# Scores as steps: each score bank keeps the scores of two key tiles ago

## The reference

```python
xq = einsum('bsh,oh->bso', x, wq).reshape(bsz, 16, seqlen, 64)   # k, v likewise
scores = softmax(einsum('bhid,bhjd->bhij', xq, xk) * SCALE)
out = einsum('bhij,bhjd->bhid', scores, xv).reshape(bsz, seqlen, 1024)
return einsum('bso,ho->bsh', out, wo)
```

## Time and profile before

| | us |
|---|---|
| median of three runs | 1537.33 (1533.9 to 1538.94) |
| the profiled execution, its own time | 1539.9 |
| its span, first to last instruction | 1538.1 |
| mean granted TensorE clock | 0.977 of full |

### The profile page before, as it was taken

The page is one execution under the profiler, slowest core; times in us unless marked ns, Lnnn a source line. Parts: engine busy times, 40 slices in busy tenths (PEclk is TensorE's granted clock), DMA queues, the critical chain, the costliest instruction groups (busy, mean ns, idle before and its releaser), DMA issues.

```text
span 1538.1 us, 23944 instructions
## 1 busy us (share of the span) xinstructions
PE 1475.9 (96%) x8778; PEld 803.9 (52%) x8778; DVE 936.0 (61%) x1017; ACT 650.2 (42%) x785; POOL 1197.4 (78%) x534
## 2 busy tenths in 40 slices
PE   5899999999999999999999999999999999998898
PEld 4455545555555555554555555554555555544555
DVE  4556666666556656666666656665666666665544
ACT  4344344444344434434444434443444444443432
POOL 1198988888789878898788878987988888976232
PEclk8799999999999999999999999999999999998999
DMA  6010101010101001010101010000101010000000
GB/s 166 1 28 1 28 1 28 1 29 1 29 1 28 1 5 25 1 28 1 28 1 28 1 29 1 15 15 1 28 1 28 1 28 1 1 1 0 8 7 14
DMA packets 22161, 24.71 MB, mean 16 GB/s; under 512 B 2730, under 2 KB 13618, under 8 KB 22066
## 3 DMA queue, kind: packets, MB, share of 16 engines
q1 hardware_dynamic: 21922, 23.28, 6.3%
q10 hardware_dynamic: 144, 0.00, 0.0%
HBM read 5.31 MB, written 1.05 MB: 4 GB/s over the span
## 4 chain that ended last, share of the span: by engine, by line
PE 83%; DVE 9%; issue 4%; POOL 2%; ACT 1%; SPq 1%; DMA 1%; DVEq 0%; POOLq 0%; ACTq 0%
PE ps L1081 26%; PE ps L1006 11%; PE ps L1056 7%; PE ps L1064 7%; PE ps L1059 7%; PE ps L1069 7%; PE ps L985 5%; DVE peak_parts L825 3%; DVE inv_sum L845 3%; PE ps L988 2%; PE ps L432 2%; PE ps L1105 2%; PE ps L433 2%; PE ps L414 2%; PE ps L1094 2%
## 5 line engine op out<-in xcount | busy, mean ns | idle before, releaser
L759 POOL TENSOR_TENSOR acc<-acc,probs 128x1024 f32<-128x1024 f32 x448 | 1075.5, 2401 | 159.8 <-ACT probs L712 129.7
L825 DVE TENSOR_REDUCE peak_parts<-ps 128x2 f32<-128x1024 f32 x512 | 624.4, 1221 | 419.3 <-PE ps L1006 417.3
L712 ACT ACTIVATE probs<-ps 128x1024 f32<-128x1024 f32 x512 | 497.5, 1022 | 566.1 <-PE ps L1069 566.1
L1081 PE MATMUL ps<-probs,v_sb 128*64 128x512 f32 x2048 | 503.1, 607 | 0.0
L1081 PEld LDWEIGHTS ps<-probs,v_sb 128*64 128x64 f32 x2048 | 124.7, 136 | 233.0 <-issue 168.0
L1056 PE MATMUL ps<-q_hi,k_hi 64*128 64x512 f32 x512 | 204.2, 399 | 14.4 <-issue 14.4
L1069 PE MATMUL ps<-shifts,minus 64*128 64x512 f32 x1024 | 204.7, 394 | 0.0
L1056 PE MATMUL ps<-q_hi,k_swap_hi 64*128 64x512 f32 x512 | 204.1, 399 | 0.0
L1059 PE MATMUL ps<-q_lo,k_hi 64*128 64x512 f32 x512 | 202.7, 396 | 0.0
L1064 PE MATMUL ps<-q_hi,k_lo 64*128 64x512 f32 x512 | 202.6, 396 | 0.0
L1064 PE MATMUL ps<-q_hi,k_swap_lo 64*128 64x512 f32 x512 | 202.6, 396 | 0.0
(11 more groups left out here) (147 smaller groups left out, 1283.1 us busy)
## 6 DMA issues: line engine op xcount, KB each, us to landing
k_swap_hi<-k_hi SPq DMA_DIRECT2D x64, 128.0 KB, 2.3
k_swap_lo<-k_lo SPq DMA_DIRECT2D x64, 128.0 KB, 2.3
probs<-in_L_ffn_w_dram SPq DMA_DIRECT2D x2, 512.0 KB, 5.1
shifts<-shift_sb SPq DMA_DIRECT2D x64, 2.0 KB
out_dram<-probs SPq DMA_DIRECT2D x4, 256.0 KB, 2.3
x_in<-in_L_attn_x_dram SPq DMA_DIRECT2D x1, 960.0 KB, 9.2
probs<-in_L_attn_wq_dram SPq DMA_DIRECT2D x1, 512.0 KB, 4.8
probs<-in_L_attn_wk_dram SPq DMA_DIRECT2D x1, 512.0 KB, 6.4
```

The source lines that it names most:

```text
L712: act.activation(probs[:, kt % PROBS, :], ps[:, 2 * place:2 * place + 2, :].rearrange("p a b -> p (a b)"), ACT.Exp, scale=SCALE).then_inc( ...
L759: pool.tensor_tensor(total, total if kt > 1 else probs[:, 0, :], probs[:, kt % PROBS, :], ALU.add).then_inc(added, 1)
L825: dve.tensor_reduce(peak_parts[:, :, i // STRETCHES, i % STRETCHES], ps[:, bank:bank + 2, :], AX.X, ALU.max).then_inc(peak_free, 1)
L1081: mm = pe.matmul(ps[at:at + HEAD_DIM, PV_BANK, :], v_sb[:, p, chunk_of(kt) * HEAD_DIM:(chunk_of(kt) + 1) * HEAD_DIM], probs[:, kt % PROBS, ...
```

## The change

A tile's scores are no longer computed from nothing. The bank still holds the finished scores of the tile two before (exp only reads it), maxima already taken off, and the matmuls of the new tile add the *difference*: q times (k of this tile minus k of the tile two before). So:
- `key_tile` is renumbered, so that tile `kt` and tile `kt - 2` are neighbours in the same row half.
- For each k projection ScalarE keeps, beside k_hi, an exact copy in `k_raw`, whose first 128 columns are zero. DVE subtracts `k_raw`, read 128 columns earlier, from the projection in PSUM (`step_k`, place 8 or 12) into `d_raw` and frees the bank. ScalarE rounds `d_raw` into `d_hi` (`round_step`), and DVE subtracts once more, `d_lo = d_raw - d_hi` (`low_k`), both at place 10 or 16. k_lo and k_swap_lo are gone; SP swaps the halves of d_hi and of d_lo (`swap_d`). k_hi stays, for the pairs.
- `scores` uses d_hi and d_lo, starts a fresh accumulation for tiles 0 and 1 only, and adds `minus` times `shifts` for these two only.
- The prologue gets the same jobs; there the swaps of d stand behind the loads of the experts' weights.

```diff
-LOW_PLACES = ({4: ("low q", 0), 8: ("low k", 0), 12: ("low k", 1)}, {4: ("low q", 1)})
+LOW_PLACES = ({4: ("low q", 0), 8: ("step k", 0), 10: ("low k", 0), 12: ("step k", 1), 16: ("low k", 1)},
+              {4: ("low q", 1)})
@@ key_tile
-    return kt // 8, kt % 4, kt % 8 // 4
+    return kt // 8, kt % 8 // 2, kt % 2
@@ SP
-            for i in (0, 1):
-                swap_lo(Job(1 + i), i, 0)
...
+            for i in (0, 1):
+                swap_d(i + 1, d_hi_ready, i, 0, d_hi, d_swap_hi)
+                swap_d(i + 1, d_lo_ready, i, 0, d_lo, d_swap_lo)
@@ ScalarE, side
                     act.copy((q_hi if kind == "q" else k_hi)[:, parity, cols], job.ps).then_inc(hi_ready, 1)
+                    if kind == "k":
+                        act.copy(k_raw[:, P + i * BANK:P + (i + 1) * BANK], job.ps).then_inc(raw_ready, 1)
...
+            def round_step(job, i, parity):
+                act.wait_ge(job_free, job.full)
+                act.copy(d_hi[:, parity, i * BANK:(i + 1) * BANK], d_raw[:, i, :]).then_inc(d_hi_ready, 1)
@@ VectorE
+            def step_k(job, i, copies):
+                dve.wait_ge(raw_ready, copies)
+                dve.tensor_tensor(d_raw[:, i, :], job.ps, k_raw[:, i * BANK:(i + 1) * BANK],
+                                  ALU.subtract).then_inc(job_free, 1)
+            def low_k(i, parity, steps):
+                cols = slice(i * BANK, (i + 1) * BANK)
+                dve.wait_ge(d_hi_ready, steps)
+                dve.tensor_tensor(d_lo[:, parity, cols], d_raw[:, i, :], d_hi[:, parity, cols],
+                                  ALU.subtract).then_inc(d_lo_ready, 1)
@@ TensorE, scores
-                hi = [k_hi, k_swap_hi] if odd == 0 else [k_swap_hi, k_hi]
-                lo = [k_lo, k_swap_lo] if odd == 0 else [k_swap_lo, k_lo]
+                hi = [d_hi, d_swap_hi] if odd == 0 else [d_swap_hi, d_hi]
+                lo = [d_lo, d_swap_lo] if odd == 0 else [d_swap_lo, d_lo]
...
+                if kt == 0 and half == 0:
+                    pe.wait_ge(swapped_d, head * D_SWAPS + D_SWAPS)
                 for b in range(2):
                     pe.matmul(ps[:, slot + b, :], hi[b][at[b], p, cols], q_hi[at[b], p, q],
-                              start=True, stop=False, tile_position=(b * HEAD_DIM, 0))
+                              start=kt < 2, stop=False, tile_position=(b * HEAD_DIM, 0), skip_group_check=True)
...
-                if kt == 0:
-                    pe.wait_ge(shift_ready, unit * 32 + 32)
-                for b in range(2):
-                    mm = pe.matmul(ps[:, slot + b, :], minus[at[b], :], shifts[at[b], half, :],
-                                   start=False, stop=True, tile_position=(b * HEAD_DIM, 0))
+                if kt < 2:
+                    if kt == 0:
+                        pe.wait_ge(shift_ready, unit * 32 + 32)
+                    for b in range(2):
+                        mm = pe.matmul(ps[:, slot + b, :], minus[at[b], :], shifts[at[b], half, :],
+                                       start=False, stop=True, tile_position=(b * HEAD_DIM, 0), skip_group_check=True)
```

More of the change, by code:

```diff
@@ L114, in build @@
         k_hi = sb("k_hi", [P, 2, HALF], F32R)
-        k_lo = sb("k_lo", [P, 2, HALF], F32R)
         k_swap_hi = sb("k_swap_hi", [P, 2, HALF], F32R)
-        k_swap_lo = sb("k_swap_lo", [P, 2, HALF], F32R)
+        d_hi = sb("d_hi", [P, 2, HALF], F32R)
+        d_lo = sb("d_lo", [P, 2, HALF], F32R)
+        d_swap_hi = sb("d_swap_hi", [P, 2, HALF], F32R)
+        d_swap_lo = sb("d_swap_lo", [P, 2, HALF], F32R)
+        d_raw = sb("d_raw", [P, 2, BANK])
+        k_raw = sb("k_raw", [P, P + HALF])
         shifts = sb("shifts", [P, 2, BANK], F32R)
@@ L179, in build @@
         hi_ready = sem("hi_ready")
[L180 removed]
+        raw_ready, d_hi_ready, d_lo_ready = sem("raw_ready"), sem("d_hi_ready"), sem("d_lo_ready")
+        swapped_hi, swapped_d = sem("swapped_hi"), sem("swapped_d")
         peak_ready = sem("peak_ready")
@@ L233, in units @@
                     yield p, half, t * 2 + p, t * 4 + (2 * p + half), plan
-        PROLOGUE = PROJECTIONS[:3] + [("pair", i) for i in range(8)] + PROJECTIONS[3:4] \
+        PROLOGUE = PROJECTIONS[:3] + [("pair", i) for i in range(8)] + [("low k", 0), ("low k", 1)] \
+            + PROJECTIONS[3:4] \
             + [("pair", i) for i in range(8, PEAK_PAIRS)] + [("shift", 0)] + PROJECTIONS[4:] \
@@ L606, in body @@
                                     swap_hi(head * CASTS + (CASTS + 2 + i), i, 1 - p)
-                                    swap_lo(Job(jobs_at(t) + local), i, 1 - p)
+                                if kind == "low k":
+                                    swap_d(head * 2 + (3 + i), d_hi_ready, i, 1 - p, d_hi, d_swap_hi)
+                                    swap_d(head * 2 + (3 + i), d_lo_ready, i, 1 - p, d_lo, d_swap_lo)
                                 if kind == "shift":
@@ L717, in body @@
                                     side(Job(jobs_at(t) + local), kind, i, 1 - p)
+                                if kind == "k":
+                                    k_jobs[i] = Job(jobs_at(t) + local)
+                                if kind == "low k":
+                                    round_step(k_jobs[i], i, 1 - p)
                                 if kind in ("turn", "logits"):
@@ L871, in _ @@
                     pair(i % PEAK_PAIRS, i, i // PEAK_PAIRS, PEAK_BANK - i % 2 * 2)
-                if kind in ("q", "k"):
-                    low(Job(jobs, PROLOGUE_BANKS[jobs]), kind, i, 0, PROJECTIONS.index((kind, i)) + 1)
+                if kind == "q":
+                    low_q(Job(jobs, PROLOGUE_BANKS[jobs]), i, 0, PROJECTIONS.index((kind, i)) + 1)
+                if kind == "k":
+                    step_k(Job(jobs, PROLOGUE_BANKS[jobs]), i, i + 1)
+                if kind == "low k":
+                    low_k(i, 0, i + 1)
                 if kind == "shift":
@@ L895, in body @@
                                     pair(i, target * PEAK_PAIRS + i, target, PEAK_BANK)
-                                if kind in ("low q", "low k"):
-                                    low(Job(jobs_at(t) + (local - 1)), kind[-1], i, 1 - p,
-                                        head * CASTS + (CASTS + PROJECTIONS.index((kind[-1], i)) + 1))
+                                if kind == "low q":
+                                    low_q(Job(jobs_at(t) + (local - 1)), i, 1 - p,
+                                          head * CASTS + (CASTS + PROJECTIONS.index(("q", i)) + 1))
+                                if kind == "step k":
+                                    step_k(Job(jobs_at(t) + (local - 1)), i, head * 2 + (3 + i))
+                                if kind == "low k":
+                                    low_k(i, 1 - p, head * 2 + (3 + i))
                                 if kind == "inv":
```

29 lines of the change are left out of this document (15 added, 14 removed).

## The result

| | before | after |
|---|---|---|
| median of five runs, us | 1537.96 (1533.9 to 1542.48) | 1550.59 (1546.62 to 1553.82) |
| the profiled execution, its own time | 1539.9 | 1553.82 |
| its span | 1538.1 | 1552.0 |
| mean granted TensorE clock | 0.977 | 0.965 |

The account below looks back on a forecast made before the run. PE was taken to bind plain steps, DVE by a little places 16 to 23. Gains of 33, 4, 3, 2 and losses of 43, 1, 8 made 10 us slower, rounded to 9: 1546 us, range 1505 to 1568.

Parts of the forecast that it names:

- The removal and the bank wait: Plain steps: 102 us of PE work removed, but the bank's 1.83 us keeps steps at 4.12; gain 33 us.
- Rival (d): Plain steps: the bank wait does not bind and d_lo is hidden, full 102 us come off; 1435 us; chance 0.03.
- Second halves: Places 16 to 23 of second halves: about 9.1 us instead of 9.38, gain 0.3 times 15, 4 us.
- The d_lo of place 16: First halves: DVE's subtraction waits for POOL's add, PE idles 2.6 us; loss 3.05 times 14, 43 us.
- rival (a): Place 16: d_lo slips in ahead of POOL's add of tile 8, loss 0.94 instead of 3.05; 1507 us; chance 0.22.
- Rival (b): d_lo's lock by POOL costs only the mean of the scaling L853, 1657 ns; 1525 us; chance 0.12.
- Per first half: Each of 14 first halves: 1.15 us gained in plain steps, 3.05 lost at place 16, 0.6 for the clock.
- The clock: After PE's idle of 2.6 us per head, matmuls may run at half rate; loss 0.6 per head, 8 us.
- Rival (c): Half rate follows each PE stall and nothing hides it; 1570 us; chance 0.13.
- Unit 0: The first unit was given a loss of 1 us.
- The tail: Last head, where most pairs or jobs are missing: gain 3 us, though POOL binds its end.
- the prologue: Swaps leave SP's queue ahead of the FFN weights: 1 us of gain, 2 either way.

Follow-up runs that it names:

- two: Kernel before with the matmuls of minus and shifts left out for tiles 2 to 15, maxima not subtracted there; 1497.74 us, ratio 0.9719.
- four: Kernel before without the minus and shifts matmuls for tiles 2 to 15, and DVE's maxima over 256 of 512 keys per bank; 1429.05 us, ratio 0.9263.
- one: Changed kernel with both d_lo, their roundings and swaps moved to places 6 and 10 of the head's second half; 1498.48 us, ratio 0.9725.
- three: Changed kernel with the matmuls of minus and shifts kept for every tile; 1588.62 us, ratio 1.0297.
- five: Changed kernel with the second d_lo at place 15 instead of 16, ahead of the reciprocal; 1510.09 us, ratio 0.9794.
- nine: Kernel before with PE's order within a step changed to scores, weighing, pair, scores, weighing, pair; 1609.43 us, ratio 1.0456.
- ten: Changed kernel with both d_lo at second-half places 6 and 10, and that half's reciprocal 3 and scaling at 19 and 21; 1526.0 us, ratio 0.9896.

## Why the prediction was right, step by step

- **The removal and the bank wait.** Foretold 1.83, 0.43, a step of 4.12 and the ceiling of 102 us cut to about 37 with places 16 to 23. Measured 4.13, and 43 us by the removal alone. Rival (d) is refuted by two (1498 and not 1435), and four shows what held it back.
- **Second halves.** Foretold 9.1 from B of place 15 to B of place 23, measured 9.13; foretold 1.45 gained per unit, measured 20.0 / 15 = 1.3.
- **The d_lo of place 16.** Foretold: DVE may start at B + 2.93, ends at + 5.50, B of place 19 at + 6.72 after 2.6 of idle, A of place 21 at + 9.5, B of place 23 at 13.8 to 14.2. Measured 2.95, 5.48, 6.67 after 2.49, 9.42, 14.19. The change in phase of rival (a) did not happen: it was 2.5 us in every head of the loop. Rival (b), the mean price, fails on the 2.53 at 841.89, and its mean of 1.94 hides the split: about 1.6 at place 10 and 2.5 at place 16. B of place 23 came at 13.9 to 14.3 in twelve heads and at 16.18 in the two with a long stretch at half rate. The later scaling was blocked in some heads (2.86 at 848.23) and not in others (0.67 at 253.57); the next point but one says why.
- **Per first half** 1.15 gained, 3.05 lost and 0.6 for the clock make +2.5, or 35 us; measured +33.7.
- **The clock.** Between 75 and 1350 us the granted clock falls to 0.5 in 14 stretches after, in 5 before. Windows of after, the granted clock third last, behind two such waits and, as the third, behind the wait of 2.49 before 845.61:

```profile
169.00:172.00 3.00, 2.85 (x16) 1.47 (x14) 3.00 (x4) 2.01 (x2) 1.56 (x2) 0.55 0.18 40
592.50:595.50 3.00, 2.71 (x12) 2.17 (x14) 3.00 (x5) 0.45 (x1) 1.30 (x1) 0.51 0.40 93
846.00:849.00 3.00, 2.14 (x18) 1.27 (x16) 3.00 (x4) 1.94 (x2) 1.45 (x2) 1.00 0.24 55
```

  Waits of the same length (2.41 before 168.37, 2.49 before 592.79, 2.49 before 845.61) were followed by half rate twice and by full rate once; of the 14 waits at place 16, 2.41 to 2.49 long, nine were. I had charged every head 0.6. In fact a single short stretch costs nearly nothing (the interval stays at 43.7), for two reasons. The next pair waits for DVE anyway, so A of place 21 comes only 0.2 to 0.4 later. And at half rate the exp comes later too, so POOL's next add starts behind the scaling and not just ahead of it:

```profile
595.41 0.67 DVE L894 TENSOR_TENSOR oT<-o_raw,inv_sum 128x512 f32<-128x512 f32 x1
596.24 4.79 POOL L785 TENSOR_TENSOR acc<-acc,probs 128x1024 f32<-128x1024 f32 x2 [2.43 <-ACT probs L734]
...
848.18 5.12 POOL L785 TENSOR_TENSOR acc<-acc,probs 128x1024 f32<-128x1024 f32 x2 [1.55 <-ACT probs L734]
```

  At full rate the add begins at 848.18, the scaling 0.05 later, and it takes 2.86; at half rate it goes first and takes 0.67. Six of the seven heads with a short stretch behind the wait have this, and B of place 23 comes at 13.9 to 14.1 in them against 14.2. I had seen this race (9.3 beside 9.28) but not that the clock decides it. Two longer stretches of 6.8 us cost 2.0 each (45.7). With three at loop boundaries (intervals of 49.4 to 49.6 instead of 48.2 to 48.4), less the 1.5 of the one that before had there, this is about 6 us against my 8. Rival (c), 1570, has the mechanism but forgets what hides it.
- **Where a size was off.** The terms of the sum as they stand make 10, and 9 was taken; unrounded they make 9.3. Unit 0: I gave a loss of 1, it gained 1.7, because no output is scaled there yet and its own d_lo took 0.96 at 86.77. The tail: I gave the last head a gain of 3; its interval gained 1.7, and from the last mark to the end the profiled execution lost 4.8. Against the forecast the tail with the last interval is 6.1 worse (+3.1 for -3), unit 0 is 2.7 better, the second halves are 1.8 worse, the first halves 1.3 better and the prologue 0.8 worse: 4.7 together, which is the distance of the profiled 13.9 from 9.3. Between the medians the distance is 3.9. That it is so small is partly luck: the tail's miss of 6 meets misses the other way. Some of the tail belongs to this one execution: one, three and five, with the same code there, take 194.6 to 195.0 from the last mark to the end, and not 197.0. Part of it is seen: the layernorm's twelve instructions on DVE (1360.61 before, 1369.06 after) took 11.3 us instead of 9.5, and the mean granted clock of the last 142 us is 0.93 against 0.96 before. Why the clock is lower there was not tried and stays open.

## What to carry to other kernels

Before counting the matmuls that an edit removes, measure in the timeline how long the shared bank takes from one writer to the next (here 1.83 us): the saving ends there, and of 102 us here 43 were left. A DVE instruction with two SBUF inputs beside a busy GpSimd has no price of its own; here (128x512, float32) it costs 0.69 us when no add runs and otherwise until the end of the running add plus 0.55 us. So it belongs where nothing is queued behind it, and its place must be chosen by when it arrives and not by DVE's busy share. A change that adds such work should be tried at other places of the queue before it is judged: here the same instructions gave 1551, 1510 and 1498 us.

## What the runs showed of the hardware

- One more change from matmuls on two row halves to matmuls on two column halves and back costs 0.39 us, about 0.2 each way (nine: a step of 4.74 against 4.35). A weighing whose second block was split off took 1.00 us for that block, as long as both blocks of a tile together (1.01 in nine, half of 1.86 in the earlier trace rows).
- A wait of PE of 2.4 to 2.5 us can be followed by half rate (1.2 GHz) and need not be: nine of 14 were. In ten a wait of 1.76 was followed by it. The short stretches cost less than their length suggests, because a kernel that waits for DVE already has slack on PE, and because the later exp let DVE's scaling go ahead of POOL's add.
- An instruction of DVE that reads two SBUF tensors and begins during a POOL add ends 0.55 to 0.56 us after it, at whatever point of the add it begins (55 of 55 in the trace of after). Only the scalings of five that begin 0.05 to 0.06 before an add's end take their own 0.67.
- In these timelines a matmul whose wait ends before its predecessor's modelled end shows no idle time at all (815.80). The 0.12 us that PE waits in each plain step of this change show only in the distance of the starts.
